# Hybrid attention chain on one core: another order of units and banks, with small-tile matmuls in runs of at most 96 records

## The chip, the core and the metric

The kernel runs on one core of a Trainium2 chip. The time is that of the device in microseconds: before the change the median of three runs is 3141.79 us (3138.49 to 3148.79). The engines are named as in the profile: PE (TensorE, matmuls), PEld (its weight loads), DVE (VectorE), ACT (ScalarE), POOL (GpSimd) and SP (SyncE, which issues the DMAs).

## The reference

x has the shape (4, 2048, 512) in float32. Four residual steps follow each other, each on a layer norm of x:

```python
x = x + attn_a(layernorm(x))   # linear attention, 16 heads of 64, q and k through relu + eps,
                               # running sums of k and of k v^T along the sequence, output projection Wo, bias
x = x + ffn(layernorm(x))      # rows and columns rounded to int8, integer product with rhs (512 x 512), scaled back
x = x + attn_b(layernorm(x))   # q, k, v, gate projections, rotary turn, 16 heads with rank-16 keys,
                               # M = M * decay + g k v^T ; y = q M ; output projection ; x + out ; layer norm
x = x + ffn(layernorm(x))      # the same rhs again
```

attn_a and attn_b are recurrent along the 2048 rows; the kernel computes them chunk by chunk: inside a chunk of 128 rows with masked score matrices, between chunks with a state that is carried on.

## The kernel before, in words

There are 64 chunks of 128 rows (16 per batch element). All weights stay on chip: float32 weights are split into a high and a low fp16 half in the prologue, and a product is then three fp16 matmuls (`three_pass`, L771 to L773).

The work on a chunk is cut into some 110 named steps. Of these the following are PE's, with the matmul records of one chunk in the trace:

- `v0`, `v1` (12 records of 512 columns each), `qk0` to `qk3` (48 of 128 columns each): projections of attn_a; `kt0`, `kt1`: transposes of k (L729).
- in 64x64 tiles: `s` (L836, 64 records), the scores; `so0`, `so1` (L850, 32 each), queries times state; `o0`, `o1` (L868, 32 each), scores times v into the same banks; `u0`, `u1` (L883, 32 each), the state update. `wo0`, `wo1`: 24 long matmuls in all, the output projection of attn_a.
- `mm0`, `mm1` (L912): the integer products, 4 records of 512 columns in bf16.
- `qb`, `kb`, `vb`, `gb`, `qr`, `kr`, `kT`: projections of attn_b; in small tiles `ys0`, `ys1` (L1004, 16 records each), `sb` (L980, 64), `yb` (L1021, 64, tiles 64x32) and `ub` (L1036, 32, tiles 64x32); `out` (L1049, 8 records, float32 128x512), its output projection.

A matmul of float32 small tiles shows as two records in the trace where the program has one; each record has a weight load of its own. 448 records of a chunk are small-tile ones.

The other engines have steps for evictions, masks, norms and rounding: `mm0_e` (DVE, L1422), `mm0_a` (POOL, L667, adds the result to x), `nb_st`, `nb_rs`, `nb_ap` (layer norm of attn_b: moments on DVE, rsqrt on POOL, `xnb` at L1298 on DVE), `s_e` (DVE, L1338, masks the scores for `o0` and `o1`), `xTa_t`, `xTb_t` (SP, transposing DMAs of the normed rows), `ld_t` (SP, rotary table), `st_o` (SP, store of the result).

**What sets the order.** The list `ORDER` holds (step, lag) pairs. The program is a sequence of slots; in slot n every engine walks the whole list and does each step of its own for chunk n - lag. So each engine's instruction stream is the list restricted to its steps, and several chunks are in work at once. The engines meet only through semaphores: `take` waits until a bank is free, `filled` until it is written. `BANK` says in which of the 8 PSUM banks a unit's result lies. The first `FIRST_LOOP_SLOT = 2 * MAX_LAG + 2` slots are unrolled, since their waits differ and pieces of the weight preparation stand between their steps (`LATE` says behind which step of which slot; `BORROWED` which bank a piece uses). Then a loop runs whose body is two slots. In it waits compare with registers computed per iteration (`COUNTS`). `MAX_LAG` unrolled slots drain the rest. With `MAX_LAG` 4 that is 10 unrolled slots, 27 iterations and 4 more slots. The loop's end is a jump back on every engine:

```python
for s in range(FIRST_LOOP_SLOT):
    walk(Slot(eng, s))
with nc.Fori(FIRST_LOOP_SLOT // 2, CHUNKS // 2, engines=[eng.engine], hint_back_edge=True) as it:
    registers = {(per, const): eng.snap(it * per + const) for per, const in COUNTS[name_of]}
    for n in range(2):
        walk(Slot(eng, n, it, registers))
for s in range(CHUNKS, CHUNKS + MAX_LAG):
    walk(Slot(eng, s))
```

PE's order in a slot before, with small-tile runs in brackets: v0, [so0, so1, o0, o1: 128 records], qk2, qb, kb, gb, wo0, wo1, qk3, qk0, vb, kr, qk1, [ub: 32], kT, qr, kt1, mm1, mm0, kt0, [ys0, sb, ys1: 96], v1, [yb, s, u1, u0: 192], out. Behind out every second slot has the jump back.

Of the kernel before, what the change touches and what calls it, by code (L numbers as in the profile page):

```python
# [90 lines left out]
AHEAD = ("ld_x", "na_st", "na_rs", "na_ap", "xTa_h", "xTa_l", "xTa_t")  # L93

LATE = {
    (0, "aT0_t"): ("load o",),
    (0, "qb_a"): ("max o", "turn decay"),
    (0, "nf1_ap"): ("all o",),
    (0, "nb_rs"): ("scale o",),
    (0, "ld_t"): ("hi o",),  # L100
    (0, "u0"): ("keep decay",),
    (1, "so0"): ("lo o",),
    (1, "qk2"): ("load rq",),
    (1, "nf1_ap"): ("load rhs",),
    (1, "na_rs"): ("load bk",),
    (1, "sb_e0"): ("max rhs",),
    (1, "ld_t"): ("all rhs",),
    (1, "s_e"): ("columns of rhs", "rows of rhs"),
    (2, "v0"): ("scale rhs",),
    (2, "u1_e"): ("round rhs",),  # L110
    (2, "qk2"): ("load g",),
    (2, "aT1_h"): ("max bk",),
    (2, "no_ap"): ("load bq", "all bk"),
    (2, "nf1_rs"): ("scale bk", "hi bk"),
    (2, "gb"): ("max bq",),
    (2, "wo1"): ("lo bk",),
    (2, "gb_s"): ("all bq",),
    (2, "kb_h"): ("load rk",),
    (2, "nf0_rs"): ("max g",),
    (2, "rnd1"): ("scale bq",),  # L120
    (2, "rnd0"): ("all g",),
    (2, "na_st"): ("hi bq",),
    (2, "kT_e"): ("lo bq",),
    (2, "sb_e0"): ("scale g",),
    (2, "v1"): ("load bv",),
    (2, "xTa_l"): ("max rk",),
    (2, "ld_t"): ("all rk",),
    (2, "s_e"): ("hi g",),
    (3, "u1_e"): ("max rq",),
    (3, "so1"): ("scale rk",),  # L130
    (3, "qk2"): ("max bv",),
    (3, "qb"): ("all rq", "hi rk"),
    (3, "no_rs"): ("lo g",),
    (3, "kb"): ("scale rq",),
    (3, "qk2_e"): ("all bv",),
    (3, "nf1_rs"): ("lo rk",),
    (3, "qb_a"): ("hi rq",),
    (3, "nf1_ap"): ("scale bv",),
    (3, "nf1_q"): ("lo rq", "hi bv"),
    (3, "nf0_rs"): ("lo bv",),  # L140
    (3, "rnd0"): ("load wout",),
# [4 lines left out]
BORROWED = {"decay": (0, "qb_a", 5),
            "o": (0, "nf1_ap", 0),
            "rhs": (1, "ld_t", 3),
            "rhs rows": (1, "s_e", 2),
            "bk": (2, "no_ap", 1),  # L150
            "bq": (2, "gb_s", 3),
            "g": (2, "rnd0", 1),
            "rk": (2, "ld_t", 3),
            "rq": (3, "qb", 4),
            "bv": (3, "qk2_e", 4)}
# [12 lines left out]


COUNTS = {  # L170
    "SP": [(2, -3), (2, -2), (2, -1), (2, 0), (2, 1), (8, -4), (8, 0), (10, -14), (10, -9), (10, -5), (10, -4),
           (10, 0)],
    "POOL": [(2, -3), (2, -2), (2, -1), (2, 0), (2, 1), (2, 2), (6, -7), (6, -4), (6, -1), (8, -5), (8, -4), (8, -1),
# [6 lines left out]
    "ACT": [(2, -3), (2, -2), (2, -1), (2, 0), (2, 1), (2, 2), (6, -4), (6, -1), (6, 2), (8, -6), (8, -5), (8, -3),  # L180
           (8, -2), (8, -1), (8, 1), (10, -11), (10, -9), (10, -8), (10, -7), (10, -6), (10, -4), (10, -3), (10, -2),
           (10, -1), (10, 2), (32, 0), (32, 16)],
    "DVE": [(2, -3), (2, -2), (2, -1), (2, 0), (2, 1), (2, 2), (4, -3), (4, -2), (4, -1), (4, 0), (6, -5), (6, -3),
# [1435 lines left out]
```

How the kernel before makes its waits and increments, by code:

```python
    def wait(self, sem, count):  # L200
        per, const = count
        if const <= self.waited.get(sem.name, 0 if per == 0 else -10 ** 9):
            return
        self.waited[sem.name] = const
        if per == 0:
            self.eng.wait_ge(sem, const)
        else:
            self.eng.wait_ge(sem, self.registers[count])
# [297 lines left out]
        def taken(eng, n):  # L506
            eng.wait_ge(s_read, TAKEN.index(n) + 1)
# [3 lines left out]
        @block.sync  # L512
# [71 lines left out]
                sp.dma_start(row[:, :], src.rearrange("(a n) -> a n", a=1).to_broadcast([P, src.shape[0]]))\  # L584
                    .then_inc(s_row, 16)
            xTa_t(first_chunk(sp, "xTa_t"))
            run(sp, "SP", dict(ld_x=ld_x, ld_t=ld_t, st_o=st_o, xTa_t=xTa_t, aT0_t=aT_t(0), aT1_t=aT_t(1), xTb_t=xTb_t,
                         qT0_t=qT_t(0), qT1_t=qT_t(1)),
                {"load o": lambda: load("o", Wo, "k"), "load rhs": lambda: load("rhs", rhs, "o"),
                 "load bk": lambda: load("bk", k_w, "o"), "load bq": lambda: load("bq", q_w, "rhs"),
                 "load g": lambda: load("g", g_w), "load bv": lambda: load("bv", v_w, "bq"),
                 "load rk": lambda: load("rk", ranks[1]), "load rq": lambda: load("rq", ranks[0]),
                 "load wout": load_wout})
            sp.wait_ge(out_free, 16 * CHUNKS)
# [1 line left out]
        @block.gpsimd  # L596
# [22 lines left out]
            pool.memset(va[:, :, DA:VA], 1.0).then_inc(s_pool, 1)
            pool.wait_ge(s_pool, 10)
```

## Time and profile before

| | |
|---|---|
| median of 3 runs | 3141.79 us (3138.49 to 3148.79) |
| the profiled execution | 3145.69 us, of which 3142.8 us are the span shown |
| PE | 2945.4 us busy (94% of the span), 54866 matmul records |
| PEld | 2207.3 us (70%) |
| DVE | 2220.4 us (71%) |
| POOL, ACT | 1045.4 us (33%), 647.1 us (21%) |
| mean granted clock of PE | 0.991 |
| DMA | 153.91 MB, 49 GB/s mean |

The page of the profile gives busy time per engine, the span in 40 slices, the DMA queues, the chain of work that ended last, the costliest groups of instructions and the DMA issues. A queue called "instruction" moves the program itself. In the chain, "issue" is time in which an engine waited for nothing that the profile shows. Matmul ends are modelled: a record of a small tile is shown some 0.22 us long although the next starts 0.012 to 0.017 us behind it, so rates are read from the distances of starts. "PEldq" is the sequencer of PE, on which its branches run. Line numbers are those of the kernel before; those of the changed kernel are higher by 2 behind the head of the file.

### The profile page before, as it was taken

The numbers are of one execution on the slowest core, as the hardware profiler recorded it, in microseconds if no ns is written. First come the engines' busy times: TensorE is split into PE (matmuls) and PEld (weight loads), VectorE is DVE, ScalarE is ACT, GpSimd is POOL, SyncE is SP. The second block draws the span as 40 slices with busy tenths as digits, with TensorE's granted clock in tenths as the row PEclk, the third lists the DMA queues.
The fourth block names the chain that finished last, engine by engine and source line by source line (L and its number), as shares of the span: only waits on it lengthen the run. The fifth ranks groups of instructions, "written<-read, shape, count | busy, mean of one in ns | idle before, by whom it ended". The sixth has DMA issues, their size and how long they took to land.

```text
span 3142.8 us, 126343 instructions
## 1 busy us (share of the span) xinstructions
PE 2945.4 (94%) x54866; PEld 2207.3 (70%) x54932; DVE 2220.4 (71%) x4958; ACT 647.1 (21%) x1165; POOL 1045.4 (33%) x1520
## 2 busy tenths in 40 slices
PE   3899999999999999999999999999999999999996
PEld 2677777777777777777777777777777767777674
DVE  7977777677676677676776677776766767767765
ACT  2222212212212212121212122122122122212211
POOL 2133423323333333333333233233233333333333
PEclk9999999999999999999999999999999999999998
DMA  5322222212122122122122121121121221121211
GB/s 172 79 49 48 46 45 48 46 43 48 44 44 46 44 47 43 42 48 48 42 48 48 42 48 45 44 48 44 43 46 44 47 43 43 47 48 42 48 41 31
DMA packets 384392, 153.91 MB, mean 49 GB/s; under 512 B 352800, under 2 KB 361632, under 8 KB 383904
## 3 DMA queue, kind: packets, MB, share of 16 engines
q1 hardware_dynamic: 383904, 146.05, 20.4%
q8 instruction: 472, 7.73, 1.0%
q14 instruction: 16, 0.13, 0.0%
HBM read 45.32 MB, written 16.78 MB: 20 GB/s over the span
## 4 chain that ended last, share of the span: by engine, by line
PE 92%; issue 4%; DVE 2%; DMA 1%; ACT 0%; POOL 0%; SPq 0%; POOLq 0%; DVEq 0%; ACTq 0%
PE bank L771 22%; PE bank L773 21%; PE bank L772 21%; PE bank L1049 7%; PE bank L912 3%; PE bank L729 2%; PE bank L850 2%; PE bank L836 2%; PE bank L868 2%; PE bank L883 2%; PE bank L980 2%; PE bank L1021 2%; PE bank L1004 1%; PE bank L1036 1%; DMA work<-in_L_attn_a_Wk 0%
## 5 line engine op out<-in xcount | busy, mean ns | idle before, releaser
L653 POOL TENSOR_TENSOR var_eps<-mean_var,column 128x1 f32<-128x1 f32 x320 | 107.2, 335 | 1362.7 <-DVE mean_var L1293 1362.7
L771 PE MATMUL bank<-xaT,wk_hi 128*128 128x128 f16 x2048 | 361.5, 221 | 0.0
L772 PE MATMUL bank<-xaT,wk_hi 128*128 128x128 f16 x2048 | 361.3, 221 | 0.0
L773 PE MATMUL bank<-xaT,wk_lo 128*128 128x128 f16 x2048 | 361.1, 221 | 0.0
L771 PE MATMUL bank<-xaT,wq_hi 128*128 128x128 f16 x2048 | 360.1, 220 | 0.0
L773 PE MATMUL bank<-xaT,wq_lo 128*128 128x128 f16 x2048 | 360.0, 220 | 0.0
L772 PE MATMUL bank<-xaT,wq_hi 128*128 128x128 f16 x2048 | 359.7, 220 | 0.0
L771 PE MATMUL bank<-xbT,wb 128*128 128x128 f16 x2048 | 346.6, 219 | 1.3 <-DMA xbT<-work 1.3
L772 PE MATMUL bank<-xbT,wb 128*128 128x128 f16 x2048 | 346.6, 219 | 0.0
L773 PE MATMUL bank<-xbT,wb 128*128 128x128 f16 x2048 | 346.5, 219 | 0.0
L771 PEld LDWEIGHTS bank<-xaT,wq_hi 128*128 128x128 f16 x2048 | 201.4, 98 | 62.6 <-issue 52.5
L1049 PE MATMUL bank<-wout,work 128*128 128x512 f32 x512 | 238.9, 609 | 2.3 <-ACT work L1150 1.7
L1106 ACT ACTIVATE work<-work 128x512 f16<-128x512 f32 x128 | 80.7, 630 | 777.7 <-DVE work L1360 777.7
L1327 DVE TENSOR_SCALAR work<-bank,column 128x256 f32<-128x256 f32 x512 | 222.4, 476 | 8.0 <-PE bank L773 3.7
L695 POOL TENSOR_TENSOR middle_b<-state_b,column 128x128 f32<-128x128 f32 x64 | 25.6, 401 | 584.4 <-DVE u_tmp L1486 584.4
L772 PEld LDWEIGHTS bank<-xaT,wq_hi 128*128 128x128 f16 x2048 | 201.6, 98 | 7.6
L771 PEld LDWEIGHTS bank<-xaT,wk_hi 128*128 128x128 f16 x2048 | 202.4, 99 | 0.1
L772 PEld LDWEIGHTS bank<-xaT,wk_hi 128*128 128x128 f16 x2048 | 202.4, 99 | 0.0
L773 PEld LDWEIGHTS bank<-xaT,wk_lo 128*128 128x128 f16 x2048 | 202.3, 99 | 0.0
L771 PEld LDWEIGHTS bank<-xbT,wb 128*128 128x128 f16 x2048 | 200.5, 98 | 2.3 <-issue 2.1
L773 PEld LDWEIGHTS bank<-xaT,wq_lo 128*128 128x128 f16 x2048 | 201.7, 98 | 0.0
L772 PEld LDWEIGHTS bank<-xbT,wb 128*128 128x128 f16 x2048 | 200.5, 98 | 0.0
(204 smaller groups left out, 8086.3 us busy)
## 6 DMA issues: line engine op xcount, KB each, us to landing
xin<-in_L_attn_a_x SPq DMA_DIRECT2D x64, 256.0 KB, 2.6
out<-work SPq DMA_DIRECT2D x64, 256.0 KB, 2.0
table<-in_tables SPq DMA_DIRECT2D x64, 192.5 KB, 2.5
work<-in_L_attn_a_Wq SPq DMA_DIRECT2D x1, 2048.0 KB, 8.6
work<-in_L_attn_a_Wk SPq DMA_DIRECT2D x1, 2048.0 KB, 14.2
wb<-in_L_attn_a_Wv SPq DMA_DIRECT2D x1, 2048.0 KB, 18.8
work<-in_L_attn_a_Wo SPq DMA_DIRECT2D x1, 2048.0 KB, 8.1
work<-work SPq DMA_TRANSPOSE x128, 2.7
```

The source lines that it names most:

```text
L653: pool.tensor_tensor(var_eps[n][:, one], mean_var[n][:, c.par, 1:2], eps[:, :], ALU.add)\
L729: last = nc.tensor.transpose(bank[:, i * P:(i + 1) * P], src(i), id_)
L771: nc.tensor.matmul(o, a[0], b[0], start=first, stop=False)
L772: nc.tensor.matmul(o, a[0], b[1], start=False, stop=False)
L773: return nc.tensor.matmul(o, a[1], b[0], start=False, stop=last)
L836: last = nc.tensor.matmul(bank[half_of(h), HALF * m:HALF * m + HALF], qk[half_of(p), 1, m, half_of(h)], qk[half_of(p), 0, m, half_of(h)], ...
L850: last = nc.tensor.matmul(bank[out_half(p, h), i * VA:(i + 1) * VA], qk[half_of(p), 0, m, half_of(h)], state[half_of(p), m, :], start=i == ...
L868: last = nc.tensor.matmul(bank[out_half(p, h), i * VA:(i + 1) * VA], sc[g][half_of(h), p, i, :], va[half_of(h), 2 * m + p, :], start=False ...
L912: last = nc.tensor.matmul(bank[:, :], xqT[w][:, k, :], rhs_q[:, k, :], start=k == 0, stop=k == KD - 1)
L1049: last = nc.tensor.matmul(bank[:, :], yT[:, k, :], wout[:, k, :], start=k == 0, stop=k == KD - 1)
L1106: nc.scalar.activation(a_split[g][:, 0, :].rearrange("p (m h e) -> p m h e", m=4, h=2), attn[:, 4 * g:4 * g + 4, :, :], ACT.Copy).then_inc ...
L1327: last = nc.vector.tensor_scalar(qk[:, n, m, :].rearrange("p m t -> p (m t)"), bank[:, 256 * n:256 * n + 256], 0.0, e_[:, :], ALU.max, ALU ...
```

## The change

The list, the banks and the tables that follow from them are replaced; no step's own code is changed. The lines that set the structure, cut to the core:

```diff
-ORDER = [("x2l", 4), ("u0_e", 2), ("xTa_t", 1), ("xTb_l", 3), ("v0", 1), ("bias", 2), ("u1_e", 2), ("so0", 2),
+ORDER = [("s", 2), ("so1", 2), ("nb_rs", 3), ("ld_t", 3), ("nb_ap", 3), ("xTb_h", 3), ("s_e", 2), ("xTb_l", 3),
+         ("x2l", 4), ("xTb_t", 3), ("out_e", 4), ("qk0", 1), ("so0", 2), ("o1", 2), ("o0", 2), ("o0_e", 2),
...
-         ("nb_ap", 2), ("y_e", 3), ("ld_t", 2), ("u1", 1), ("u0", 1), ("s_e", 1), ("xTb_h", 2), ("out", 3)]
+         ("u0", 1), ("u1", 1), ("mm0_e", 2), ("u0_e", 1), ("mm1_a", 4), ("u1_e", 1), ("mm0_a", 2), ("out", 3),
+         ("nb_st", 2), ("xTa_t", 0)]
...
-BANK = {"v0": 6, "v1": 4, "qk0": 2, "qk1": 0, "qk2": 3, "qk3": 5, "kt0": 6, "s_a": 6, "s_b": 7, "o0a": 1, "o0b": 0,
+BANK = {"v0": 7, "v1": 7, "qk0": 6, "qk1": 7, "qk2": 6, "qk3": 0, "kt0": 3, "s_a": 7, "s_b": 1, "o0a": 2, "o0b": 3,
...
 LATE = {
-    (0, "aT0_t"): ("load o",),
+    (0, "qk1_e"): ("load o",),
...
-BORROWED = {"decay": (0, "qb_a", 5),
+BORROWED = {"decay": (0, "qb_e", 0),
...
 COUNTS = {
-    "SP": [(2, -3), (2, -2), (2, -1), (2, 0), (2, 1), (8, -4), (8, 0), (10, -14), (10, -9), (10, -5), (10, -4),
+    "SP": [(2, -4), (2, -3), (2, -2), (2, -1), (2, 0), (2, 1), (2, 2), (8, -9), (8, -8), (8, -5), (8, -4), (8, -1),
```

`st_o` has lag 5 now, so `MAX_LAG` is 5: 12 slots are unrolled ahead of the loop, the loop has 26 iterations, and 5 slots drain. Only `st_o` has that lag. The loop body has 3,523 PE instructions (before: 3,514).

PE's order in a slot is now, with small-tile runs in brackets: [s, so1: 96], qk0, [so0, o1, o0: 96], qk1, qk3, kb, qb, qk2, gb, wo0, wo1, vb, kr, kt0, qr, [ub: 32], kT, v0, [ys0, sb, ys1: 96], kt1, v1, mm1, [yb: 64], mm0, [u0, u1: 64], out. `s` follows `out` across the slot's edge, with lag 2 in place of 1, which is the same chunk.

On PE at the loop's entry the kernel before has, behind the last slot of the prologue (v1, then yb L1021, s L836, u1 and u0 L883, out L1049; L489 is the loop, L208 a register count):

```order
L773 MATMUL bank<-wv_hi,xaT 128x512
L1021 MATMUL bank<-work 32x64 x32
L836 MATMUL bank<-work 64x64 x32
L883 MATMUL bank<-va,work 64x65 x32
L1049 MATMUL bank<-wout,work 128x512 x4
L489 UNCONDITIONAL_BRANCH
L489 BRANCH_PREFETCH_HINT
L489 ISA
L208 REGISTER_ALU
L771 MATMUL bank<-wv_hi,xaT 128x512
...
L850 MATMUL bank<-state_a,work 64x65 x2
L850 MATMUL bank<-middle_a,work 64x65 x2
```

The changed kernel has at the same place (L914 is mm1 and then mm0, L1023 yb, L885 u, L1051 out, L838 s, L852 so1, L773 the first matmul of qk0):

```order
L775 MATMUL bank<-wv_hi,xaT 128x512
L914 MATMUL bank<-rhs_q,xqT 128x512 x4
L1023 MATMUL bank<-work 32x64 x32
L914 MATMUL bank<-rhs_q,xqT 128x512 x4
L885 MATMUL bank<-va,work 64x65 x32
L1051 MATMUL bank<-wout,work 128x512 x4
L491 UNCONDITIONAL_BRANCH
L491 BRANCH_PREFETCH_HINT
...
L210 REGISTER_ALU x2
L838 MATMUL bank<-work 64x64 x32
...
L852 MATMUL bank<-state_a,work 64x65 x2
...
L773 MATMUL bank<-xaT,wq_hi 128x128
```

The scores moved from ahead of u to behind the jump, v0 no longer opens the loop, and mm1 and mm0 now part yb from v1 and from u.

On DVE around the end of the loop body the kernel before has (L1422 mm1_e and mm0_e, L1298 na_ap and nb_ap, L1479 sb_e, L1290 to L1293 nb_st, L1318 the low half of the rows for attn_a, L1338 s_e):

```order
L1422 SCALAR_TENSOR_TENSOR work<-bank,row_scale,rs_row 128x512
L1422 SCALAR_TENSOR_TENSOR xf<-bank,row_scale,rs_row 128x512
L1298 TENSOR_SCALAR xna<-xin,mean_var,rstd 128x512
L1479 TENSOR_TENSOR work<-bank,causal 128x256 x4
L1290 BN_STATS stats<-xwb 128x6
L1292 COPY column<-column 128x1
L1293 BN_AGGR mean_var<-stats 128x2
L1318 TENSOR_TENSOR xa_split<-xna,xa_split 128x512
L1298 TENSOR_SCALAR xnb<-xwb,mean_var,rstd 128x512
L1338 TENSOR_TENSOR work<-bank,causal 128x2x256 x2
```

The changed kernel has at the loop's entry (L1424 mm1_e and mm0_e, L1374 and L1378 u_e, L1292 to L1295 nb_st, L1300 nb_ap, L1340 s_e, L1314 the low half of xnb):

```order
L1424 SCALAR_TENSOR_TENSOR work<-bank,row_scale,rs_row 128x512
L1424 SCALAR_TENSOR_TENSOR xf<-bank,row_scale,rs_row 128x512
L1374 TENSOR_TENSOR middle_a<-state_a,bank 128x260
L1378 SCALAR_TENSOR_TENSOR state_a<-middle_a,keep_a,bank 128x260
...
L1292 BN_STATS stats<-xwb 128x6
L1294 COPY column<-column 128x1
L1295 BN_AGGR mean_var<-stats 128x2
L491 UNCONDITIONAL_BRANCH
...
L1300 TENSOR_SCALAR xnb<-xwb,mean_var,rstd 128x512
...
L1340 TENSOR_TENSOR work<-bank,causal 128x2x256
...
L1314 TENSOR_TENSOR work<-xnb,work 128x512
```

mm0_e and nb_st now stand directly ahead of the jump, with the state's update between them, and nb_ap and s_e directly behind it.

## Rows read from the trace of the kernel before

**Rows 1.** Page, part 4: the chain that ended last, shares of the span.
```profile
PE 92%; issue 4%; DVE 2%; DMA 1%; ACT 0%; POOL 0%; SPq 0%; POOLq 0%; DVEq 0%; ACTq 0%
```

**Rows 2.** PE's waits from 530 to 3010 us: us in total, times, longest.
```profile
PE bank L868 <- issue: 45.3, 26, 2.2
PE bank L836 <- issue: 24.4, 26, 1.2
PE bank L883 <- issue: 22.9, 26, 1.2
```

**Rows 3.** Windows between successive gaps: us, busy (x records) PE, PEld, DVE, ACT, POOL.
```profile
1494.29:1531.24 36.95, 35.94 (x627) 28.29 (x627) 27.08 (x59) 9.20 (x18) 13.44 (x20) 1.00 0.22 50
1531.24:1578.19 46.95, 45.66 (x878) 34.43 (x880) 34.13 (x78) 9.75 (x19) 16.59 (x24) 1.00 0.22 46
1578.19:1589.72 11.53, 9.64 (x212) 5.82 (x211) 5.81 (x16) 0.63 (x1) 2.09 (x4) 1.00 0.16 27
```

**Rows 4.** Page, part 3: the queue that brings the program; packets, MB, share.
```profile
q8 instruction: 472, 7.73, 1.0%
```

**Rows 5.** Chain from 1570 to 1598 us, across a jump back.
```profile
1579.35 3.63 PE bank L1049 x8
...
1586.78 1.05 PE bank L868 x63
1587.82 1.89 issue
```

**Rows 6.** Line L489 (the loop) on PE's sequencer: ns min/median/max, first and last start.
```profile
L489 PEldq COMPARE_BRANCH  x27: 88/2869/3173, 529.2 to 3010.4; - x27
```

**Rows 7.** DMA queues from 1579.4 to 1579.6 us: packets, MB, share.
```profile
q8 instruction: 1, 0.02, 36.4%
```

**Rows 8.** DMA queues from 1583.0 to 1583.2 us.
```profile
q1 hardware_dynamic: 215, 0.06, 120.9%
q8 instruction: 1, 0.02, 35.2%
```

**Rows 9.** Windows behind a gap: us, busy PE, PEld, DVE, ACT, POOL, PEclk, DMA, GB/s.
```profile
1590.64:1594.05 3.41, 3.41 (x36) 3.41 (x33) 3.33 (x6) 1.12 (x2) 0.00 (x0) 0.50 0.20 47
```

**Rows 10.** Timeline of PE, 1528 to 1532 us: start, us, line, operation, count.
```profile
1528.06 0.38 PE L772 MATMUL bank<-wv_lo,xaT 128*128 128x512 f16 x1
1528.27 0.38 PE L773 MATMUL bank<-wv_hi,xaT 128*128 128x512 f16 x1
1528.58 0.86 PE L1021 MATMUL bank<-work 64*32 64x64 f32 x64
1529.37 0.92 PE L836 MATMUL bank<-work 64*64 64x64 f32 x44
1531.24 0.51 PE L836 MATMUL bank<-work 64*64 64x64 f32 x18 [0.96 <-issue]
```

**Rows 11.** Timeline of PE, 1589.7 to 1590 us.
```profile
1589.71 0.21 PE L868 MATMUL bank<-va,work 64*64 64x65 f32 x1 [1.89 <-issue]
1589.86 0.23 PE L771 MATMUL bank<-xaT,wq_hi 128*128 128x128 f16 x1
1589.92 0.22 PE L772 MATMUL bank<-xaT,wq_hi 128*128 128x128 f16 x1
```

**Rows 12.** Lines of DVE: busy us, mean ns, idle before.
```profile
L1298 DVE TENSOR_SCALAR xnb<-xwb,mean_var,rstd 128x512 f32<-128x512 f32 x64 | 90.4, 1412 | 50.4 <-POOL rstd L656 50.4
...
L1338 DVE TENSOR_TENSOR work<-bank,causal 128x512 f32<-128x512 f32 x128 | 82.0, 681 | 31.9 <-PE bank L836 31.9
...
L1422 DVE SCALAR_TENSOR_TENSOR work<-bank,row_scale,rs_row 128x512 f32<-128x512 f32 x64 | 48.0, 751 | 41.8 <-PE bank L912 41.8
```

**Rows 13.** Lines of POOL: busy us, mean ns, idle before.
```profile
L667 POOL TENSOR_TENSOR xwb<-xwa,xf 128x512 f32<-128x512 f32 x64 | 82.0, 1281 | 13.3 <-DVE xf L1422 4.4
```

**Rows 14.** Timeline of SP's DMA issues, 1525 to 1527 us.
```profile
1525.51 0.35 SPq L548 DMA_DIRECT2D out<-work  x1
1526.35 0.34 SPq L544 DMA_DIRECT2D table<-in_tables  x1
```

More of the change, by code:

```diff
@@ L49 @@
 MAGIC = 1.5 * 2.0 ** 23
-ORDER = [("x2l", 4), ("u0_e", 2), ("xTa_t", 1), ("xTb_l", 3), ("v0", 1), ("bias", 2), ("u1_e", 2), ("so0", 2),
[4 rows of a table removed]
-         ("kb_a", 3), ("v0_e", 1), ("gb_e", 3), ("gb_s", 3), ("nf1_q", 4), ("wo_e", 2), ("nf0_st", 2), ("gb_k", 3),
[7 rows of a table removed]
-         ("nb_ap", 2), ("y_e", 3), ("ld_t", 2), ("u1", 1), ("u0", 1), ("s_e", 1), ("xTb_h", 2), ("out", 3)]
+ORDER = [("s", 2), ("so1", 2), ("nb_rs", 3), ("ld_t", 3), ("nb_ap", 3), ("xTb_h", 3), ("s_e", 2), ("xTb_l", 3),
+         ("x2l", 4), ("xTb_t", 3), ("out_e", 4), ("qk0", 1), ("so0", 2), ("o1", 2), ("o0", 2), ("o0_e", 2),
+         ("qk1", 1), ("o1_e", 2), ("qk3", 1), ("kb", 3), ("aT0_h", 2), ("aT0_l", 2), ("qb", 3), ("aT1_h", 2),
+         ("qk0_e", 1), ("bias", 2), ("no_st", 4), ("no_rs", 4), ("st_o", 5), ("aT0_t", 2), ("no_ap", 4),
+         ("aT1_l", 2), ("no_f", 4), ("nf1_st", 4), ("qk2", 1), ("kb_e", 3), ("aT1_t", 2), ("qk1_e", 1),
+         ("nf1_rs", 4), ("gb", 3), ("nf1_ap", 4), ("qb_e", 3), ("kb_a", 3), ("gb_e", 3), ("kb_h", 3), ("gb_s", 3),
[8 rows of a table added]
+         ("nb_st", 2), ("xTa_t", 0)]
 LAG = dict(ORDER)
@@ L70 @@
 MAX_LAG = max(LAG.values())
-BANK = {"v0": 6, "v1": 4, "qk0": 2, "qk1": 0, "qk2": 3, "qk3": 5, "kt0": 6, "s_a": 6, "s_b": 7, "o0a": 1, "o0b": 0,
-        "u0a": 0, "u0b": 4, "kt1": 7, "o1a": 4, "o1b": 5, "u1a": 1, "u1b": 5, "wo": 2, "mm0": 4, "qb": 7, "kb": 5,
-        "vb": 7, "gb": 0, "qr": 2, "kr": 3, "sb0": 0, "sb1": 7, "sb2": 5, "sb3": 1, "y0": 2, "y1": 3, "ub0": 6,
-        "ub1": 4, "out": 2, "mm1": 1}
+BANK = {"v0": 7, "v1": 7, "qk0": 6, "qk1": 7, "qk2": 6, "qk3": 0, "kt0": 3, "s_a": 7, "s_b": 1, "o0a": 2, "o0b": 3,
+        "u0a": 2, "u0b": 6, "kt1": 6, "o1a": 4, "o1b": 5, "u1a": 3, "u1b": 4, "wo": 1, "mm0": 5, "qb": 3, "kb": 2,
+        "vb": 2, "gb": 4, "qr": 4, "kr": 0, "sb0": 3, "sb1": 5, "sb2": 2, "sb3": 4, "y0": 0, "y1": 1, "ub0": 5,
+        "ub1": 1, "out": 0, "mm1": 4}
 BANKS = 8
@@ L95 @@
 LATE = {
-    (0, "aT0_t"): ("load o",),
[L97 to L141, printed above, removed]
+    (0, "qk1_e"): ("load o",),
@@ new lines @@
+    (0, "nf1_ap"): ("max o",),
+    (0, "qb_e"): ("turn decay",),
+    (0, "qb_a"): ("all o",),
+    (0, "sb"): ("scale o",),
+    (0, "xTa_l"): ("hi o", "keep decay"),
+    (1, "no_st"): ("lo o",),
+    (1, "no_ap"): ("load g",),
+    (1, "nf1_q"): ("load rk",),
+    (1, "ld_x"): ("load rhs",),
+    (1, "xTa_l"): ("max rhs",),
+    (1, "u1"): ("all rhs",),
+    (1, "u0_e"): ("columns of rhs",),
+    (1, "u1_e"): ("rows of rhs",),
+    (1, "mm0_a"): ("load bk",),
+    (2, "nb_rs"): ("scale rhs",),
@@ new lines @@
+    (2, "xTb_t"): ("round rhs",),
+    (2, "qb"): ("load rq",),
+    (2, "bias"): ("load bq",),
+    (2, "aT1_l"): ("max bk",),
+    (2, "nf1_rs"): ("all bk",),
+    (2, "wo0"): ("scale bk", "max bq"),
+    (2, "qk3_e"): ("max g",),
+    (2, "wo_e"): ("all g", "max rk"),
+    (2, "kr"): ("all bq",),
+    (2, "ld_x"): ("scale bq",),
+    (2, "kT"): ("scale g",),
+    (2, "kt0_e"): ("hi bk",),
+    (2, "ub_m"): ("all rk",),
+    (2, "kT_e"): ("hi bq",),
+    (2, "ys1"): ("scale rk",),
+    (2, "sb_e0"): ("max rq",),
@@ L142 @@
+    (2, "na_ap"): ("lo bk",),
+    (2, "u1_e"): ("all rq",),
+    (2, "out"): ("hi g",),
+    (2, "nb_st"): ("lo bq", "hi rk"),
+    (3, "nb_rs"): ("load bv",),
+    (3, "xTb_t"): ("scale rq",),
+    (3, "qk3"): ("hi rq", "lo g"),
+    (3, "bias"): ("lo rk",),
+    (3, "no_rs"): ("max bv", "all bv"),
+    (3, "qk1_e"): ("scale bv",),
+    (3, "nf1_rs"): ("lo rq",),
+    (3, "nf1_ap"): ("hi bv",),
+    (3, "kb_h"): ("lo bv",),
+    (3, "qb_a"): ("load wout",),
 }
 TAKEN = ("q", "k", "v", "o", "rhs", "bk", "bq", "g", "rk", "rq", "bv")
-BORROWED = {"decay": (0, "qb_a", 5),
[L147 to L155, printed above, removed]
+BORROWED = {"decay": (0, "qb_e", 0),
+            "o": (0, "qb_a", 4),
+            "rhs": (1, "u1", 5),
+            "rhs rows": (1, "u1_e", 6),
+            "bk": (2, "nf1_rs", 3),
+            "g": (2, "wo_e", 0),
+            "bq": (2, "kr", 1),
+            "rk": (2, "ub_m", 1),
+            "rq": (2, "u1_e", 0),
+            "bv": (3, "no_rs", 5)}
@@ L170 @@
 COUNTS = {
-    "SP": [(2, -3), (2, -2), (2, -1), (2, 0), (2, 1), (8, -4), (8, 0), (10, -14), (10, -9), (10, -5), (10, -4),
-           (10, 0)],
-    "POOL": [(2, -3), (2, -2), (2, -1), (2, 0), (2, 1), (2, 2), (6, -7), (6, -4), (6, -1), (8, -5), (8, -4), (8, -1),
[6 rows of a table removed]
[L180 to L183, printed above, removed]
[4 rows of a table removed]
+    "SP": [(2, -4), (2, -3), (2, -2), (2, -1), (2, 0), (2, 1), (2, 2), (8, -9), (8, -8), (8, -5), (8, -4), (8, -1),
+           (12, -17), (12, -11)],
+    "POOL": [(2, -3), (2, -2), (2, -1), (2, 0), (2, 1), (2, 2), (8, -7), (8, -6), (8, -4), (8, -3), (8, -2), (8, 0),
[6 rows of a table added]
+    "ACT": [(2, -3), (2, -2), (2, -1), (2, 0), (2, 1), (2, 2), (8, -10), (8, -8), (8, -7), (8, -6), (8, -4), (8, -3),
[3 rows of a table added]
+    "DVE": [(2, -4), (2, -3), (2, -2), (2, -1), (2, 0), (2, 1), (2, 2), (4, -3), (4, -2), (4, -1), (4, 0), (8, -7),
[4 rows of a table added]
 }
```

41 rows, old and new, of tables (COUNTS, ORDER) are left out of this document.

## The prediction

> **What bounds the kernel now.** I read the chain of waits first: TensorE's matmuls are 92% of it, and the only other entry of size, "issue", is 4% [rows 1], time in which PE waited for nothing that the profile shows. VectorE's 71% therefore bounds nothing; what counts is the sum of PE's work and PE's gaps. Then PE's waits in the loop, cut to its 26 full bodies (530 to 3010 us): three lines with 26 waits each and nothing else of size, together 92.6 us [rows 2]. Each body of two slots (about 95.4 us) has the same three gaps: in the score matmuls (L836), between scores and state update (L883), and at the last record of L868. All lie in runs of small-tile matmuls.
>
> Why there? Cut at three successive gaps, the body holds 627 matmuls and 627 weight loads, then 878 and 880 [rows 3]. With PE's register, wait and branch instructions from the program's listing these are 1,280 and 1,790 (7 x 256 = 1,792; two records are missing): the gaps are multiples of 256 instructions apart. The third stretch, 442 instructions, goes over the back edge, which jumps 3,514 back: 442 - 3,514 = -12 x 256. And the instruction queue moved 472 packets of 7.73 MB [rows 4], 16 KB each. So PE receives its program in blocks of 256 instructions and stalls when it reaches the end of one before the next has landed. A 128-column matmul and its load use up two instructions in 0.056 us (1589.86 to 1589.92 in rows 11), so a block lasts 7 us in projections; a small-tile record follows its neighbour after 0.017 us (63 of L868 in 1.05, rows 5), so 128 of them use a block up in about 2 us. At 1530 us a gap of 0.96 us lies behind 44 of L836's 64 records [rows 10], while of a body's two L868 runs only one has a gap (26 in 26 bodies). Where the loop jumps back, 63 records of L868 pass and then 1.89 us are lost [rows 5].
>
> How long is a block in coming? The gap ends at 1578.19, a packet moves inside 1579.4 to 1579.6, PE's branch, a median 2.869 us long, ends near 1582.0, and the next packet lies in 1583.0 to 1583.2 [rows 6 to 8], and PE, with v0 in hand, uses that block by 1585.5. Thus a packet starts some 1.3 us behind entry into a block and is usable 2.5 us later: 3.8 to 4.0 us a block, one block ahead only.
>
> The Trainium skill ("Runtime: NRT & Kernel Launch", Instruction fetch mechanics) agrees on blocks of 16 KiB, and says that sequential prefetch is hidden and a taken branch stalls only outside its window. Here rows 2 and 6 show gaps without any branch; by the page alone the gaps would not be there, and the change would bring only its mode changes (+20 us below).
>
> **The change part by part.** The sum is made on the profiled span, 3142.8 us.
>
> *Gaps removed.* 128 to 192 small-tile records in a row (256 to 384 instructions in 2 to 3 us) become at most 96, with 2.7 us units of long matmuls between them. In a slot without the back edge I count, from the program's listing, every 256-instruction boundary at least 4.1 us behind the one before; so these gaps go. The rows give 92.6 us; the profile's ends of matmuls are modelled 0.2 us late, so each gap is really about 0.17 us longer (L836's 44 records start at 1529.37, the 45th would have at 1530.07 and came at 1531.24: 1.17 against 0.96, rows 10). 78 gaps x 0.17 = 13, 106 in 26 bodies, and x 27/26 for the loop's first body, ahead of the window: **-110 us**. Some 4 us of such waits stand in the prologue's last slots and go too: **-4**. One boundary has only 4.1 us; if 4.3 are needed it costs 0.2 x 26 = 5.
>
> *Clock.* Behind some gaps a stretch of 3.41 us runs at the granted clock 0.50, 1.2 of 2.4 GHz [rows 9]; stepping through the loop I find six, each costing half its length: **-10 us** if the gaps go, 0 if the joint keeps causing them.
>
> *Mode changes.* The last 512-column matmul ahead of a tile run is followed by it 0.31 us later (1528.27 to 1528.58), where its pitch is 0.216 (1528.06 to 1528.27) [rows 10]: 0.093. Leaving, 0.15 passes where a record takes 0.017 [rows 11]: 0.133. A change of tile shape inside a run (yb to s) costs the 0.133 too. Before there are four runs and one inner change a chunk, afterwards six runs: 2 x (0.093 + 0.133) - 0.133 = 0.32 us, x 64 = **+20 us**. Nothing hides it, PE being the bound; bounds 13 (0.1 a run and inner change alike) to 30.
>
> The Trainium skill ("TensorEngine Tiling (Array Packing)", Key Properties) says a change of tiling mode drains the array; that speaks against this change, and the trace agrees with 0.093 and 0.133 us.
>
> *The joint.* ("Joint" is the place where the loop jumps back.) This is the largest new term. The loop now opens with s and so1 directly behind the branch, not with v0's 2.68 us. Counting PE's instructions from the program's start, the loop begins 5 instructions ahead of a boundary (before: 39). So the branch lands in a block of which 5 instructions are left, and s stands in the next. (a) The block with the branch begins 48 records into yb; behind it lie 16 yb, mm0 (0.9), u0 and u1 (1.06) and out (3.63, rows 5): 6.3 us with mode changes. The branch is over 3.8 us after entry, 2.5 before out ends; the next block is usable 3.5 later (1582.0 to 1585.5): s comes 1.0 late, plus its wait and mode change, 1.3. Bounds 0.7 (branch as early as the shortest fetch allows) to 2.4. (b) The next block holds s, so1 and 28 of qk0's 48 pairs: 1.0 + 0.5 + 1.6 + 0.1 = 3.2 us against 4.0: 0.8 (0.1 to 1.1). (c) The next: the other 20 pairs, so0, o1, o0, 8 pairs of qk1: 1.1 + 0.5 + 1.1 + 0.1 + 0.5 = 3.3: 0.7 (0.4 to 1.0). Sum 2.8 us a body, x 26 = **+73 us** (31 to 117), and **+3** of half-speed clock.
>
> *Hidden edits.* Other banks, one slot more of unrolled prologue, st_o one slot later and the moved evictions on VectorE, ScalarE and POOL cost PE nothing as long as operands come in time. The closest is VectorE at the joint: between mm0 and o1 stand mm0_e 0.75, POOL's add 1.28, moments and rstd some 1.9, xnb 1.41 and two s_e of 0.68 [rows 12, 13], 6.7 and with hand-overs 8.0 us, while PE takes 1.06 + 3.6 + 1.1 + 0.5 + 2.7 + 0.5 = 9.4 from mm0's end to o1. Cover 1.4 us, more with the joint's gap. SP passes ld_t directly behind xTa_t; both are queued ahead of use. Setup before slot 0 stays; prologue and drain: 0, bounds -5 to +8.
>
> Sum: 3142.8 - 110 - 4 - 10 + 20 + 73 + 3 = 3115. The run lasts 2.9 us longer than its span (3145.7), and that run lay 3.9 above the median of the three: **3114 us**, 0.9% faster.
>
> **The rivals.**
> *The joint is nearly free* (chance 0.13). PE's queue may run far enough ahead that the branch block is entered early; before, the branch's 2.9 us were wholly covered by out and v0. Against it: now nothing long follows it. Joint 0 to 1.5 us a body: 3040 to 3085, about 3065.
> *The joint is dearer, and the change slower* (0.17). At 1525.51 and 1526.35 SP issues the store and the table load [rows 14], and the program packet due near 1526.7 moves only after them, behind 1528.6: 1.9 us late. If one of the joint's three fetches meets such a transfer each body, or the wait sets the half clock each time (3.41 us at 0.50 loses 1.7), that is 1.7 to 1.9 x 26 = 44 to 49 us: 3160. It decides from 1.4 us a body above my 2.8. For it: SP now issues xTa_t and ld_t at the slot's edge. Against: SP runs ahead of PE by several us, and a transposing transfer did not hold back the packet in rows 8, which moved among 215 of its packets.
> *A new operand wait* (0.10). If scores or the transposed xb come 1 us late to o1 or kb, every chunk pays: 64 us, 3178. Against: 1.4 us of cover and the joint's own gap ahead of it.
> That the change does not do what it says I rule out from the listing: no run has over 96 records.
> *Only the mode changes.* If something else than the arrival of the program made the gaps and they stayed, the 20 us would come on top: 3162. The spacing by 256 leaves this no chance above rounding. The Trainium skill's section on fetch, with its hidden prefetch, points the same way and falls with it.
>
> **How the numbers follow.** The forecast's case has 0.60, its own range 3093 to 3136 (joint 2 to 3.6 us). A measurement tells about 0.3%, 9.4 us: 3132.4 to 3151.2 is "same". Faster: 0.57 of the forecast's case, 0.13, and 0.02 of the dearer joint = 0.72. Same: 0.03 + 0.08 + 0.03 = 0.14. Slower: 0.07 + 0.07 = 0.14. Range 3068 to 3152: below it lies 0.05, above 0.13.
>
> **What would show it.** PE's waits at L836, L868 and L885 of the changed kernel (the old numbers plus 2) should lose their 26 repetitions inside slots, and "issue" should instead stand right behind L1051 (before s), in the first third of qk0 and early in qk1, in sum about 2.8 us a body and 2 to 2.5% of the chain. Time at granted clock 0.50 should shrink. Each chunk's PE time without gaps should grow by 0.3 us. It would be wrong if "issue" stays in slot one's tile runs (the block count misplaced), if the gap behind the branch exceeds 2.4 us, or if L868 or the kb matmuls wait for VectorE or a DMA once a chunk.

## The result and the profile after

The changed kernel takes 3047.97 us (median of four runs, 3045.79 to 3050.33) against 3142.31 us before on the same chip: ratio 0.9698, 95% interval 0.9680 to 0.9716. 3114 us were forecast, with a range from 3068 to 3152. The direction was right, the gain over three times the forecast one, and the time fell in the rival that the joint (the place where the loop jumps back) is nearly free, which had a chance of 0.13.

The page of the changed kernel: PE's share, and the queue that brings the program (before: 2945.4 us and 94%, and [rows 4]).

```profile
PE 2938.6 (96%) x54804; PEld 2199.4 (72%) x54932; DVE 2268.8 (74%) x4958; ACT 655.8 (22%) x1165; POOL 1044.8 (34%) x1520
...
q8 instruction: 446, 7.31, 1.0%
```

PE is busy as long as before to 7 us in 2940; what went is idle time. 446 packets stand in place of 472. In a stretch of ten bodies this queue moves 140 packets in the changed kernel and 150 in the one before: 14 a body in place of 15. (The chain of waits of this profile broke off at the end, so its shares are not used.)

PE's waits in the changed kernel from 530 to 2900 us, all that there are; they stand against the 92.6 us of [rows 2]:

```profile
PE bank L914 <- issue: 8.1, 51, 0.2
```

The 78 gaps of the loop are gone, at L836, L868 and L883 (now L838, L870, L885) and nothing took their place. The row that is left is no wait: it stands where the trace lacks the first of mm1's or mm0's four records (x3 below), and 0.2 us is the pitch of one.

The joint in the timeline of PE: start, duration, line, operation, count.

```profile
1533.04 0.86 PE L1023 MATMUL bank<-work 64*32 64x64 f32 x64
1534.06 0.81 PE L914 MATMUL bank<-rhs_q,xqT 128*128 128x512 bf16 x3 [0.16 <-issue]
1534.80 1.16 PE L885 MATMUL bank<-va,work 64*64 64x65 f32 x64
1535.89 3.70 PE L1051 MATMUL bank<-wout,work 128*128 128x512 f32 x8
1539.52 1.16 PE L838 MATMUL bank<-work 64*64 64x64 f32 x64
```

out begins at 1535.89 and s, behind the jump, at 1539.52: 3.63 us, which is just what out takes with L771 behind it in the chain before [rows 5]. Forecast was a gap of 1.3 us here, 0.8 in qk0 and 0.7 in qk1.

The jump on PE's sequencer in the changed kernel: ns min/median/max, first and last start.

```profile
L491 PEldq COMPARE_BRANCH  x26: 88/1649/2305, 618.5 to 2911.5; - x26
```

It lasts 1.65 us (median) where it lasted 2.87 [rows 6]. The first and last start give the time of a body of two slots, the number by which all kernels are compared below: (2911.5 - 618.5) / 25 = 91.72 us, and before (3010.4 - 529.2) / 26 = 95.43. From slot 12 to slot 64 that is 26 x 3.71 = 96.5 us; the slots ahead gained 2.4 more, the drain took 4.7 longer (137.1 for 132.4), in sum the 94.2 us between the two spans.

### The profile page after: what moved, and what is told of

Its sections match the earlier page's. It is cut to its first block and busy times, and to the rows that moved or that the text cites. A ratio compares the mean times of both kernels' runs of the same rounds, so it can differ in the third digit from the quotient of the medians.

```text
span 3048.6 us, 126856 instructions
## 1 busy us (share of the span) xinstructions
PE 2938.6 (96%) x54804; PEld 2199.4 (72%) x54932; DVE 2268.8 (74%) x4958; ACT 655.8 (22%) x1165; POOL 1044.8 (34%) x1520
## 5 line engine op out<-in xcount | busy, mean ns | idle before, releaser
L655 POOL TENSOR_TENSOR var_eps<-mean_var,column 128x1 f32<-128x1 f32 x320 | 82.9, 259 | 1378.1 <-DVE mean_var L1295 1378.1
L773 PE MATMUL bank<-xaT,wq_hi 128*128 128x128 f16 x2048 | 360.6, 221 | 4.1 <-DVE work L1329 3.9
L773 PE MATMUL bank<-xaT,wk_hi 128*128 128x128 f16 x2048 | 358.5, 220 | 0.0
L773 PE MATMUL bank<-xbT,wb 128*128 128x128 f16 x2048 | 350.4, 220 | 8.2 <-DMA xbT<-work 8.2
L774 PE MATMUL bank<-xbT,wb 128*128 128x128 f16 x2048 | 350.4, 220 | 0.0
L775 PE MATMUL bank<-xbT,wb 128*128 128x128 f16 x2048 | 350.4, 220 | 0.0
L1051 PE MATMUL bank<-wout,work 128*128 128x512 f32 x512 | 236.7, 605 | 0.9 <-ACT work L1152 0.9
L682 POOL TENSOR_TENSOR work<-work 128x512 f32<-128x512 f32 x128 | 162.7, 1271 | 141.6 <-DVE work L1447 141.4
L773 PEld LDWEIGHTS bank<-xaT,wq_hi 128*128 128x128 f16 x2048 | 201.2, 98 | 13.0 <-DVE work L1329 4.1
L773 PEld LDWEIGHTS bank<-xbT,wb 128*128 128x128 f16 x2048 | 201.8, 99 | 9.1 <-issue 9.1
L658 POOL TENSOR_TENSOR rstd<-var_eps,column 128x1 f32<-128x1 f32 x320 | 198.0, 619 | 25.1
L775 PEld LDWEIGHTS bank<-xbT,wb 128*128 128x128 f16 x2048 | 201.9, 99 | 0.0
L774 PEld LDWEIGHTS bank<-xbT,wb 128*128 128x128 f16 x2048 | 201.8, 99 | 0.0
L774 PEld LDWEIGHTS bank<-xaT,wk_hi 128*128 128x128 f16 x2048 | 201.2, 98 | 0.0
```

The source lines that it names most:

```text
L655: pool.tensor_tensor(var_eps[n][:, one], mean_var[n][:, c.par, 1:2], eps[:, :], ALU.add)\
L658: pool.tensor_tensor(rstd[n][:, one], var_eps[n][:, one], half[:, :], ALU.pow).then_inc(rs[n], 1)
L682: pool.tensor_tensor(to[:, :, :, :], to[:, :, :, :], cross[:, :, ::-1, :], ALU.add)\
L773: nc.tensor.matmul(o, a[0], b[0], start=first, stop=False)
L774: nc.tensor.matmul(o, a[0], b[1], start=False, stop=False)
L775: return nc.tensor.matmul(o, a[1], b[0], start=False, stop=last)
```

## The experiments

Each experiment ran beside the kernel before on its own chip, mostly another than that of the first result (before: 3143 to 3153 us), so totals of different experiments compare to some 10 us only. Times per body repeat better: two kernels without a gap gave 91.72 and 91.71, three with the same single gap 91.98, 91.99 and 91.99.

Theory A, formed on this result, has two parts: the joint's price hangs on where the loop's first instruction lies in its 256-instruction block, and the prediction's count of that place (5 ahead of a block's end) is off by five or six, so that the loop begins at a block's start. (The first expectation therefore says 10 instructions where the count says 15.) To test it without touching any order, idle wait instructions are put ahead of PE's first matmul, where PE waits for the weights. A wait already met costs PE's sequencer nothing later, and moves every block's end:

```diff
+            for _ in range(2 * N):
+                pe.wait_ge(s_pool, 10)
             pe.wait_ge(s_pool, 10)
             for n, b in (("q", 0), ("k", 1), ("v", 2)):
                 maxima_to_rows(n, b)
```

Two such waits make one instruction, so 2 N lines give N (the gap found below at the place counted for N bears this out). With 128 of them the first jump comes when it did (618.6 us for 618.5); with 246 it comes 13 us later, with 200 8 us, so that they are no longer free there. So times per body are read beside the totals.

**The changed kernel, moved by 246, 200 and 128 instructions.**

> The changed kernel with 246 instructions more on PE ahead of the first matmul, where PE waits for the weights anyway: every 256-instruction boundary moves, and the loop now begins some 10 instructions ahead of one. Theory A (the price of the joint depends on how many instructions of the block at the jump's target are left; in the changed kernel the target lies at a block's start and not, as the prediction counted, 5 ahead of its end): gaps behind a few records of s and in the blocks after it, 1.5 to 2.8 us a body, 3088 to 3121 us. Theory B (the joint is hidden behind out wherever the boundaries lie): 3048 us, no gap in the loop.

> The changed kernel with 200 more instructions on PE ahead of the first matmul; the boundary falls into the middle of s, 55 to 61 instructions into the loop. Theory A: the block at the target covers half of s, the next is usable 3.3 us behind the branch, so a gap of 0.3 to 0.7 us a body in s: 3056 to 3066 us. Theory B: 3048 us.

> The changed kernel with 128 more instructions on PE ahead of the first matmul; the boundary falls to the end of s (127 to 133 instructions into the loop), and the block with the branch begins only inside out or the update. Theory A: s is covered, but the branch block is entered some 2 us later than in the changed kernel, so the branch ends near out's end and s or so1 waits 0.5 to 1.6 us a body: 3060 to 3090 us. Theory B: 3048 us.

Measured: 3063.58, 3111.24 and 3117.07 us, ratios to before 0.9745 (0.9722 to 0.9767), 0.9905 (0.9879 to 0.9930) and 0.9923 (0.9897 to 0.9948). The jump with 246, with 200 and with 128, in this order:

```profile
L491 PEldq COMPARE_BRANCH  x26: 87/1782/2481, 631.6 to 2924.3; - x26
```

```profile
L491 PEldq COMPARE_BRANCH  x26: 88/1954/2558, 626.9 to 2968.5; - x26
```

```profile
L491 PEldq COMPARE_BRANCH  x26: 88/3143/3343, 618.6 to 2975.2; - x26
```

A body takes 91.71, 93.66 and 94.26 us. None of Theory A's three ranges was met. With 246, where it wanted a gap, there is none: of the 15.6 us more than the changed kernel 13 are the late start. So A is wrong in that case: a target 15 instructions ahead of a block's end costs no more than one 5 ahead. With 200 and 128 the joint has a price, and the program comes in 472 packets again, one more a body (150 in ten bodies). B falls. The waits of PE from 530 to 2900 us with 200:

```profile
PE bank L838 <- issue: 18.3, 25, 1.5
PE bank L774 <- issue: 11.5, 24, 0.8
```

and its timeline behind one jump:

```profile
1566.95 0.68 PE L838 MATMUL bank<-work 64*64 64x64 f32 x27
1568.57 0.80 PE L838 MATMUL bank<-work 64*64 64x64 f32 x37 [0.94 <-issue]
```

With 128 the waits lie at the end of s and in so1:

```profile
PE bank L838 <- issue: 35.5, 29, 1.6
PE bank L852 <- issue: 5.2, 25, 0.2
```

With 200 the gap comes behind 27 records of s. With the 6 instructions ahead of s that is instruction 60 of the body, and 61 was the count for this kernel (5 - 200 + 256). So the counting of block ends, and with it the prediction's "5 instructions ahead of a boundary", was right to one instruction, and A's second part falls. What was wrong is what was said to follow from that place.

**The kernel before, moved by 63 instructions.**

> The kernel before, order unchanged, with 63 more instructions on PE ahead of the first matmul: the loop begins 24 instructions behind a boundary in place of 39 ahead of one. Theory A (position of the boundaries counts as well as the length of runs): the 1.9 us gap behind the joint goes or shrinks and the others change, 3040 to 3110 us. Theory C (the runs of 128 to 192 records cost their gaps wherever the boundaries lie, and the gain of the change is the splitting of the runs): 3130 to 3155 us.

Measured 3057.87 us, ratio 0.9718 (0.9691 to 0.9744), 91.99 us a body, 447 packets, inside Theory A's wide range. The kernel before, in its own order, gains nearly all that the change gained, by 63 idle instructions. (Its loop then begins 232 instructions ahead of a block's end and touches 14 blocks in place of 15, so 14 packets a body need no other reason here.) PE's waits in its loop, 530 to 2900 us:

```profile
PE bank L836 <- issue: 27.0, 25, 1.4
```

One gap a body in place of three. Theory C falls: most of the gaps were a matter of place. One gap in the run of 192 records stays.

**The hint off.**

```diff
-            with nc.Fori(FIRST_LOOP_SLOT // 2, CHUNKS // 2, engines=[eng.engine], hint_back_edge=True) as it:
+            with nc.Fori(FIRST_LOOP_SLOT // 2, CHUNKS // 2, engines=[eng.engine]) as it:
```

> The changed kernel with the loop's back-edge hint off (its instruction at the loop's head goes on every engine; all else is the same, PE's first score matmul still begins 5 instructions into the loop, just where a block ends). Theory D (with the hint the chip has the first instructions at the jump's target at hand, at least 15 of them, and fetches the block behind them at once, so that one block less is fetched a body and the joint costs nothing): without it 15 blocks a body instead of 14 (472 packets in place of 446), a branch of 3 us and more in place of 1.7, and a gap behind the jump of 1 to 3 us a body: 3075 to 3125 us. Theory E (the hint does nothing, the jump fetches that way by itself): 3048 us and 446 packets.

Measured 3166.73 us, ratio 1.0052 (1.0035 to 1.0069): half a per cent slower than before, and clear of the changed kernel's 0.9698. A body takes 96.67 us, 4.95 more than with the hint. The page's packets, PE's waits from 530 to 2900 us, the jump, and s behind one:

```profile
q8 instruction: 495, 8.11, 1.1%
```

```profile
PE bank L838 <- issue: 78.1, 24, 3.7
```

```profile
L491 PEldq COMPARE_BRANCH  x26: 83/3826/4374, 616.9 to 3033.6; - x26
```

```profile
1582.89 3.70 PE L1051 MATMUL bank<-wout,work 128*128 128x512 f32 x8
1590.32 1.99 PE L838 MATMUL bank<-work 64*64 64x64 f32 x64 [3.73 <-issue]
```

Between out and s now lie 3.3 us in the mean (78.1 / 24). Behind the gap shown s runs at half rate (1.99 us for 1.16): the granted clock is 0.50 from 1590.32 to 1592.31, the lower of its two levels, and it fell between 1589.0 and 1589.5, when PE had been idle since 1586.6. Read in windows of one us, the lower clock takes 53 us from the loop, 2.1 a body (part of it inside the gaps), and nothing in the changed kernel; with 3.1 us of gaps a body that covers the 4.95. D said 15 packets a body; there are 160 in ten bodies, so 16. The direction and the place are D's; the size (3166.73 us for at most 3125) and the sixteenth packet are beyond it. E falls. The hint is thus what makes the joint free in the changed kernel, where out is 3.6 us long and the jump lasts 1.65. (It was taken off on every engine at once; PE's gap is no wait for another engine in the profile.)

**The kernel before, moved by 24, 22 and 12 instructions.** The loop's first instruction then lies 15, 17 and 27 ahead of a block's end, and 39 in the kernel itself.

> The kernel before with 24 more instructions on PE ahead of the first matmul, so that the loop's first instruction lies 15 ahead of a block's end and not 39. Theory D with at least 15 instructions at hand: 14 packets a body, the 1.9 us gap behind the joint (L868) goes, the other two stay or move: 3060 to 3100 us. Rival (24 instructions change nothing, since one block's end still lies in each long run): 3130 to 3150 us.

> The kernel before with 12 more instructions on PE ahead of the first matmul: the loop begins 27 instructions ahead of a block's end. It brackets how many instructions are at hand behind a hinted jump: 14 packets a body and no gap in L868 if 27 are, 15 packets and a gap of 1.5 to 2 us there if they are not. Time 3060 to 3100 us in the first case, 3125 to 3150 us in the second.

> The kernel before with 22 more instructions on PE ahead of the first matmul: the target lies 17 instructions ahead of a block's end (15 fetched 14 packets a body, 27 fetched 15). It brackets how many instructions are at hand behind a hinted jump: with 17 or more 446 or 447 packets and some 3058 us, with 16 or fewer 472 packets and 3120 to 3175 us. No expectation which.

Measured: 24 gives 3058.56 us, ratio 0.9704 (0.9687 to 0.9720), 91.98 us a body and 447 packets; 22 gives 3125.65 us (one run), 94.55 us a body and 472 packets; 12 gives 3170.71 us (one run), 96.28 us a body and 472. The time with 24 lies 1.4 us under D's range, since the gap of L883 went as well; that with 12 has the packets of its second case, but lies 21 us above that case's range, with four gaps a body (L868 49.0 us in 25 waits, L836 40.8 in 50, L850 18.3 in 25). Their jumps, in this order:

```profile
L489 PEldq COMPARE_BRANCH  x27: 88/2709/3040, 531.6 to 2923.0; - x27
```

```profile
L489 PEldq COMPARE_BRANCH  x27: 88/2853/3258, 532.5 to 2990.8; - x27
```

```profile
L489 PEldq COMPARE_BRANCH  x27: 88/2970/3256, 533.3 to 3036.5; - x27
```

Two instructions, 22 or 24, are worth 2.6 us a body. The waits from 530 to 2900 us with 22:

```profile
PE bank L772 <- issue: 31.6, 25, 1.6
PE bank L836 <- issue: 23.4, 28, 1.4
PE bank L868 <- issue: 23.0, 25, 1.2
```

and with 24:

```profile
PE bank L836 <- issue: 26.7, 30, 1.3
```

One of the waits at L772:

```profile
1482.55 0.38 PE L771 MATMUL bank<-wv_hi,xaT 128*128 128x512 f16 x1
1484.35 0.39 PE L772 MATMUL bank<-wv_lo,xaT 128*128 128x512 f16 x1 [1.42 <-issue]
```

With 22 PE stops behind the seventh matmul of v0 (1481.25 to 1482.55; seven with their loads are 14 of the 17 instructions left in the block, the others stand at the loop's head), and again in L868. With 24 both waits are gone at once. The loop touches 15 blocks in both cases, but with 24 only 14 packets a body move. So with the hint, 15 instructions at the target are at hand without a packet of their own, and 17 are not. Whether the chip holds 16 or does something else that ends between 15 and 17, these runs do not tell.

**Two small-tile runs merged.** The changed kernel with mm0 ahead of yb:

```diff
-         ("xTa_h", 0), ("v1_e", 1), ("xTa_l", 0), ("mm1_e", 4), ("yb", 3), ("xhb", 3), ("mm0", 2), ("y_e", 3),
+         ("xTa_h", 0), ("v1_e", 1), ("xTa_l", 0), ("mm1_e", 4), ("mm0", 2), ("yb", 3), ("xhb", 3), ("y_e", 3),
```

> The changed kernel with mm0 moved from between yb and u to ahead of yb: one small-tile run of 128 records takes the place of two of 64, so one entry and one exit of the tile mode go a chunk, and an inner change of shape comes. Theory F (mode changes cost 0.226 us a run, 0.133 an inner change; a run may have 128 records as long as at most one block's end lies in it): 0.093 us a chunk less, 6 us: 3042 us. Rival G (any run over 96 records brings an issue gap back, 1 us in it): 1 us a body or a chunk more, 3070 to 3110 us.

Measured 3041.90 us, ratio 0.9652 (0.9636 to 0.9668), against 0.9698 (0.9680 to 0.9716) for the changed kernel: the fastest of all, and the intervals do not meet. Its loop has no wait of PE from 530 to 2900 us, with a run of 128 records, so G falls. A body takes (2903.5 - 615.1) / 25 = 91.54 us, 0.18 less; two chunks of 0.093 were forecast to give 0.19. (Of the 8.6 us between the two profiled spans the loop is 4.7; 3.4 lie ahead of it and were not forecast.) The run from yb to u, without a wait:

```profile
1528.58 0.86 PE L1023 MATMUL bank<-work 64*32 64x64 f32 x64
1529.37 1.16 PE L885 MATMUL bank<-va,work 64*64 64x65 f32 x64
```

**The last gap of the kernel before.** With 24 idle instructions one gap of 1.0 us a body was left in s (L836), and a store and a table load run shortly ahead of it, as in [rows 14].

```diff
-         ("so1", 2), ("out_e", 4), ("o0", 2), ("o1", 2), ("qk2", 1), ("no_st", 4), ("o0_e", 2), ("xTb_t", 3),
+         ("so1", 2), ("out_e", 4), ("o0", 2), ("o1", 2), ("qk2", 1), ("no_st", 4), ("o0_e", 2), ("xTb_t", 3), ("ld_t", 3),
...
-         ("nb_ap", 2), ("y_e", 3), ("ld_t", 2), ("u1", 1), ("u0", 1), ("s_e", 1), ("xTb_h", 2), ("out", 3)]
+         ("nb_ap", 2), ("y_e", 3), ("u1", 1), ("u0", 1), ("s_e", 1), ("xTb_h", 2), ("out", 3)]
```

The pieces of weight preparation that followed ld_t are moved to y_e. In the third kernel `("st_o", 5)` stands ahead of the moved `("ld_t", 3)` as well, in place of `("st_o", 4)` behind yb; 12 slots are then unrolled, and it takes 126 idle instructions to bring the loop to 15 ahead of a block's end.

> The kernel before, with ld_t (the table load on SP) moved from the end of the slot, where it follows the store, to behind xTb_t early in the next slot; nothing moves on PE. Theory H (a block of the program waits behind direct transfers, and store and table load together hold it back by 1.7 to 1.9 us in the tile run at the slot's end): the gap in L836 in the middle of the body (1.2 us) goes, the ones behind the jump stay or shrink: 3105 to 3125 us. Rival (the gaps come from the length of the runs alone): 3135 to 3150 us.

> The same with 24 more instructions on PE ahead of the first matmul, so that the jump's target lies 15 instructions ahead of a block's end. One gap of 1.3 to 1.5 us a body was left there, behind 46 records of s, with the store and the table load running where its block was due. Theory H: it goes or falls under 0.5 us, 3058 us less 27 bodies of 0.9 to 1.4 us: 3020 to 3035 us, faster than both the kernel before and the changed one, with its run of 192 small-tile records whole. Rival (a run of 192 records can't pass without a gap): 3050 to 3065 us.

> The kernel before with both the table load and the store moved from the slot's end into the next slot, behind xTb_t (the store gets lag 5, so 12 slots are unrolled and 26 iterations loop, as in the changed kernel); PE's order is untouched, and instructions ahead of its first matmul bring the jump's target to 15 ahead of a block's end. The table load alone was not what held the block back in s. Theory H2 (a block waits behind the store: its packet came 1.2 to 1.4 us after the store had landed): the last gap of 0.7 to 1.3 us a body in s goes, a body takes 90.6 to 91.2 us instead of 91.98, 3025 to 3040 us in all. Rival (the gap is what a run of 192 records costs): 91.9 us a body, 3050 to 3062 us.

Measured: before_ldt 3148.71 us, ratio 0.9993 (0.9984 to 1.0002); before_ldt_pad24 3054.92 us, 0.9694 (0.9681 to 0.9708); before_sto_pad 3058.24 us, 0.9702 (0.9686 to 0.9718). A body takes 95.57, 91.99 and 91.90 us, where the first stands against 95.43 and the others against 91.98. In before_ldt the gap in L836 shrank from 0.94 us (24.4 / 26) to 0.65 (16.2 / 25), and the body was no shorter for it:

```profile
PE bank L868 <- issue: 47.0, 25, 2.2
PE bank L883 <- issue: 22.6, 25, 1.4
PE bank L836 <- issue: 16.2, 25, 1.0
```

At 15 ahead of a block's end the gap stays with the table load moved (before_ldt_pad24: L836 27.2 us in 35 waits, for 26.7 in 30) and with both transfers moved (before_sto_pad), from 530 to 2900 us:

```profile
PE bank L836 <- issue: 25.1, 35, 1.0
```

H and H2 fall as to time, and all three totals lie in the ranges of the rival: whatever the store and the table load do to a fetch, taking them away gains at most 0.1 us a body. The 1.9 us that the prediction read from [rows 14] as such a delay are not borne out as a cost. The run of 192 records has a gap at both placements with 14 packets (24 and 63). Whether some placement lets it pass was not tried.

## Why the prediction was wrong

*That the arrival of the program makes PE wait in the tile runs* was right, and stronger than said. The gaps move with the count of instructions and appear where the count puts them (27 records into s with 200, seven matmuls into v0 with 22). The changed kernel has none.

*Gaps removed, -110 us.* Right. The rows' 92.6 us and the added 13 are 4.07 us of a body's 95.43. All are gone. (The 13 take 0.17 us a gap; the one example worked beside it, 1.17 against 0.96, gives 0.21, which would make 16.) But the short runs are not what removed most of them: in the order before two of the three gaps go with 24 or 63 idle instructions and no shorter run.

*Clock, -10 us.* Right. Read in windows of one us, each counted as lost by what its granted clock lacks to 1.00, the loop of the kernel before has six stretches at the granted clock 0.50, which take away 10.2 us in all; the changed kernel's loop has none.

*Mode changes, +20 us.* Right in kind. Before less its gaps and half-speed time is 95.43 - 4.07 - 0.38 = 90.98 us a body, the changed one 91.72: 0.37 a chunk, 24 us over 64, for 0.32 and 20. The same working from the kernel before with 24 idle instructions (91.98 less 1.04 of gaps and 0.20 for their late ends) gives 0.49 a chunk, 31 us, at the edge of the bound of 30; so the size is known to some 7 us only. after_mm0 measured one entry and one exit less for one inner change more: 0.09 for 0.093.

*The joint, +73 us, and +3 of clock.* This is the step that failed, and more than all of the miss: without it the sum is 3142.8 - 110 - 4 - 10 + 20 = 3039 for the span, and 3048.6 was measured. (The sum takes the joint 26 times, while 26 iterations jump back 25 times, so 70 by its own working.) Its statement was: "the branch lands in a block of which 5 instructions are left, and s stands in the next", so that s waits for one more block and the two behind it each come late. The place was counted rightly. But the kernel's back-edge hint, which I took from the listing without asking what it does, goes with the first instructions at the target being at hand without a packet of their own (how, the runs do not show; that it is so, the packets, the missing gap and the hint-off kernel do). The block with s came at once, one packet a body less was moved (14 for 15), and qk0 and qk1 did not wait either. With the hint off the same kernel pays 4.95 us a body; with it, but with 61 instructions left in place of 5, it pays 1.94. The forecast's 2.8 lies between the two. The trace before could not show the hint at work: its target lay 39 ahead of a block's end, on the dear side, and its 15 packets for a body with 14 block ends are what a jump with a fetch of its own moves. They fitted the forecast.

The remaining 10 us between 3039 and 3048.6: 4.7 are a longer drain, within the bounds given for prologue and drain (PE waits 8.2 us for the transposed xb there, for 1.3 before), and 4 or more the larger mode changes; the rest is not accounted for.

*The rivals.* "The joint is nearly free" was the case, for another reason than the one given (that PE's queue runs far ahead). The dearer joint, with transfers in the way of the fetch, did not come, and the three last experiments show that this mechanism costs at most 0.1 us a body in the order before. No new operand wait came: 530 to 2900 us have none. The chance was put too low because its reason was weighed and not its possibility: a behaviour at the joint that the trace before could not show had both ends open.

The Trainium skill ("Runtime: NRT & Kernel Launch", Instruction fetch mechanics) says that a taken branch whose target lies outside a window of two pages forces a fetch. The runs agree for a jump without hint (3.3 us of gap) and add what it leaves out: with the hint, a target 5 or 15 instructions from a block's end and 3.6 us of work queued ahead, no wait is left at the jump. Its sentence that sequential fetch is hidden did not hold in the small-tile runs of the kernel before, with 78 gaps in 26 bodies; here the measurement decides.

*What the change is worth.* The least expected: its order brings little that another place of the loop does not. The order before with 24 idle instructions has 3058.56 us at 0.9704 (0.9687 to 0.9720), the changed one 0.9698 (0.9680 to 0.9716): the intervals lie on each other. Both orders spread with the place of the loop alone, the one before over 91.98 to 96.28 us a body (24 and 12 instructions), the changed one over 91.71 to 94.26. At the best places tried the short runs bring 0.27 us a body: they save the one gap that is left (1.2) and pay for more mode changes. At bad places they lose less, 2.5 us for 4.3. So of the 3.71 us a body that the change gained, the place of the loop alone would have given 3.45 in the order before. How much of them is the place when one starts from the new order is open, since the changed kernel was not run with its loop 39 ahead of a block's end; at 61 ahead it takes 1.94 of them back.

## What to carry to other kernels

Where PE's idle time says "issue" and repeats at one record of a loop, count its instructions: if the gaps are multiples of 256 apart, the program's arrival is the bound, and a few idle instructions ahead of the loop are a cheaper experiment than another order. Try several placements before comparing two orders, for the placement alone moved these two by 2.5 and 4.3 us a body. And count the program's packets per iteration: 14 went with 91.5 to 92.0 us a body here, 15 with 93.7 to 96.3, so the odd one was worth another placement.
